# Two post-norm decoder layers on one core: the hand-written orders of the five engines replaced by a newly searched set

## The reference

```python
x = _layernorm(x + _L0_attn_ref(x, ...))            # 16 heads, window of 7 keys, a small net gives 7 weights a head
x = _layernorm(x + _L0_xattn_ref(x, ctx_1024, ...)) # one head, keys and values from ctx
x = _layernorm(x + _L0_ffn_ref(x, ...))             # 8 experts, each picks its 16 best tokens, attends among them
x = _layernorm(x + _L1_attn_ref(x, ...))            # one head of 256, scores times a decay mask
x = _layernorm(x + _L1_xattn_ref(x, ctx_1024, ...)) # argmax over ctx, then 16 heads over the chosen rows
x = _layernorm(x + _L1_ffn_ref(x, ...))             # quantised 256 -> 1024, width-3 convolution, silu, quantised back
```

## Time and profile before

| | |
|---|---|
| median of 3 executions | 1100.07 us (1093.01 to 1100.21) |
| the profiled execution | 1096.73 us, of it span 1094.9 us |
| TensorE matmul busy | 964.1 us (88%), 7038 instructions |
| TensorE weight load busy | 693.7 us (63%) |
| VectorE busy | 910.3 us (83%), 2503 instructions |
| ScalarE busy | 752.5 us (69%), 1854 instructions |
| GpSimd busy | 163.2 us (15%) |
| DMA queue of SyncE | 57.64 MB, 16.7% of 16 engines' time |
| mean granted TensorE clock | 0.947 |
| the chain that ended last | PE 68%, ACT 14%, DVE 12%, POOL 3%, issue 3% |

### The profile page before, as it was taken

One profiled execution on the slowest core, in us unless ns is written; L12 is line 12 of the kernel. 1 busy time (PEld: TensorE's weight loads), 2 busy tenths in 40 slices (PEclk: granted clock), 3 DMA queues, 4 the chain that ended last, 5 costly groups with the idle time before them and its releaser, 6 DMA issues.

```text
span 1094.9 us, 19705 instructions
## 1 busy us (share of the span) xinstructions
PE 964.1 (88%) x7038; PEld 693.7 (63%) x7038; DVE 910.3 (83%) x2503; ACT 752.5 (69%) x1854; POOL 163.2 (15%) x401
## 2 busy tenths in 40 slices
PE   5758889999999999999999999999999998887552
PEld 4536557676767676767767776768676756564331
DVE  4798776689898989898989989898999877867754
ACT  2223454768696878778787878786969795867643
POOL 2000110111112020302021211112120301010000
PEclk9878899999999999999999999999999998988865
DMA  7823021211110302030303020120212001000000
GB/s 224 325 67 106 1 87 34 63 46 42 49 58 9 98 21 86 6 101 1 106 1 90 17 81 26 45 63 20 77 40 68 10 1 30 1 20 1 10 10 10
DMA packets 36626, 58.90 MB, mean 54 GB/s; under 512 B 6784, under 2 KB 15872, under 8 KB 36016
## 3 DMA queue, kind: packets, MB, share of 16 engines
q1 hardware_dynamic: 36528, 57.64, 16.7%
HBM read 28.65 MB, written 4.19 MB: 30 GB/s over the span
## 4 chain that ended last, share of the span: by engine, by line
PE 68%; ACT 14%; DVE 12%; POOL 3%; issue 3%; DMA 0%; SPq 0%; ACTq 0%; POOLq 0%; DVEq 0%
PE bank_c L450 20%; PE bank_a L450 11%; PE banks_e L450 7%; PE bank_f L450 5%; PE bank_x L450 5%; PE bank_x L644 4%; PE bank_a L542 3%; PE bank_c L472 2%; ACT squares_out L1362 2%; ACT area_e L1559 2%; DVE x L880 2%; DVE area_a L1046 2%; PE banks_e L788 1%; PE banks_e L801 1%; ACT area_bx L1350 1%
## 5 line engine op out<-in xcount | busy, mean ns | idle before, releaser
L1284 DVE SCALAR_TENSOR_TENSOR area_f<-area_f,w_convw 128x254 f32<-128x254 f32 x256 | 111.5, 477 | 6.0 <-ACT area_f L1588 4.9
L1350 ACT ACTIVATE area_bx<-bank_x 128x512 f32<-128x512 f32 (+1 forms) x144 | 70.0, 498 | 29.3 <-PE bank_x L644 10.4
L1208 DVE TENSOR_REDUCE neg_top<-banks_e 128x8 f32<-128x1024 f32 x64 | 76.1, 1211 | 10.4 <-PE banks_e L450 10.3
L996 DVE TENSOR_TENSOR area_a<-area_a 128x512 f32<-128x512 f32 x112 | 73.4, 681 | 8.6 <-ACT area_a L1350 8.5
L1588 ACT ACTIVATE area_f<-area_f,w_convb,w_convw 128x256 f32<-128x256 f32 x128 | 69.6, 594 | 13.7 <-DVE area_f L1275 13.6
L1350 ACT ACTIVATE area_a<-bank_a 128x512 f32<-128x512 f32 (+1 forms) x80 | 44.1, 551 | 49.9 <-PE bank_a L450 28.3
L1350 ACT ACTIVATE area_bx<-bank_c 128x512 f32<-128x512 f32 x64 | 34.8, 544 | 61.3 <-PE bank_c L450 41.3
L1046 DVE TENSOR_TENSOR area_a<-area_a 128x512 f32<-128x512 f32 x112 | 74.4, 681 | 0.4
L1559 ACT ACTIVATE area_e<-banks_e 128x512 f32<-128x512 f32 x128 | 67.9, 599 | 1.3 <-PE banks_e L801 1.0
L1050 DVE TENSOR_TENSOR area_a<-area_a 128x512 f32<-128x512 f32 x96 | 65.1, 679 | 0.1
L1350 ACT ACTIVATE area_e<-banks_e 128x512 f32<-128x512 f32 (+1 forms) x80 | 45.8, 593 | 16.1 <-PE banks_e L472 5.9
(11 more groups left out here) (314 smaller groups left out, 2682.7 us busy)
## 6 DMA issues: line engine op xcount, KB each, us to landing
area_a<-area_a SPq DMA_DIRECT2D x96, 224.0 KB
area_a<-in_xT SPq DMA_DIRECT2D x16, 256.0 KB, 2.9
x<-in_x SPq DMA_DIRECT2D x16, 256.0 KB, 3.0
area_bx<-in_ctxT SPq DMA_DIRECT2D x16, 256.0 KB, 2.8
area_d<-in_ctxT SPq DMA_DIRECT2D x16, 256.0 KB, 3.0
y<-x SPq DMA_DIRECT2D x16, 256.0 KB, 2.2
w_wqkv_e<-in_wqkv_e SPq DMA_DIRECT2D x1, 3072.0 KB, 10.5
area_f<-in_raw SPq DMA_DIRECT2D x2, 1024.0 KB, 11.4
```

The costliest lines, as they stand in the source:

```text
L996: return dve.tensor_tensor(product_of(wi).rearrange("p (n t) -> p n t", t=P), qT0.rearrange("p c (b t) -> p (c b) t", t=P), kT0.rearrange( ...
L1208: dve.tensor_reduce(top[:, b, :, r:r + 2, 0].rearrange("p (par c) r -> p r c par", c=DC), banks_e[:, r:r + 2, :].rearrange("p r (c par k) ...
L1284: last = dve.scalar_tensor_tensor(c4[:, i, :, dst], h4[:, i, :, src], cwt3[:, 2 * jj + i, k:k + 1], c4[:, i, :, dst], ALU.mult, ALU.add)
L1350: return act.activation(dst, src, ACT.Copy)
```

## The change

The strings of `ORDER` are replaced for all five engines; the code of the steps, their waits, tiles and buffers stay as they are. The table's new rows, of which two stand for all:

```diff
 ORDER = {
     "PE": (
-        "AAAAASASSSSBBAAAABSABAABABBXXAASXBAAXAXBXBAAXXBBXXXXBSXABXXAASXBAXAXBXABBXAXCACXXXCXCXCCXACACXCACXACXCA"
+        "AAAAASASSBSSBAAAASBABABBAABXXAASXBAXAAXBAXABAXXBBXXXBXSXXABXASAXBAXAXBXABBXAXCACXXXCXCXCCCAXACXCACXACXCA"
...
     "SP": (
-        "ASSSSAAABSSSBSSAAABAAAACABAAAACABBACAFAAABCBCFAAACFBAAAFAAACBFBCAAAFBAAACFCBAAAFBAAACFAAACCBFBAACCFFCFFF"
+        "ASSSSSSAAABSBASASAABAABAACABAACACBAACAFBAACAFBAACAFAAABFAACABFBAACCAFAAABFAAACBFAAACBFAAABCFCAABCCCFFFFF"
```

More of the change, by code:

```diff
@@ new lines @@
+        "XFFAXAFAEAECXCAFCAAAFCAAAAAFEEAFAFFAAFFAFAFXECCCAFCFFFFFFEEXXXXXXAAXAXXFAEEEXFEEEFFBBAFFFAAFXXXXBBFFFFAA"
+        "FFXXAAFFEEACCFFAAAXFCCAAFAAAAFAFFAEXAEAAAAFCCCFFFEAFFCFFXXFXFFXXEXEXXXAAFXEFEFFAEEAEEBBFFXFFBAXAXAXBFFAA"
+        "XFFAXFAAAFFAFACCEFEFCAAXFCFAAAAAEFEAAFFAAXFAAFFFECCCAFFCFFFFFXXEEXXXXXEEXXEEFXEEAAFAFFABFXBFFFAAAXXXBBFF"
+        "AFFFAFFFXAXEAFFEACCAFACXAAAFCFAAAAAFFEEAXAAFAAAFFFECCCAFXFFFCXFFFXEEXXXXXXAAXFEEFAXFAFEEBBEEFAFFFBAAXXXF"
+        "BFFFAAXFAFFXAAAAFEAFECCFXAAAFCCAFAAFFFEAAAAEAFFAFAFEXCCCAFFFFCFFFXXXXEEAAAXXXAXXAFEEEXEFFFBXBEEFFBAAFFXX"
@@ new lines @@
+        "BXFFFFFFAAXXFAFAAFACCFEAEAFXACAACAAAAFEFEAFFAAAAXAFFFFECCCAFFFFCFFFXXXXEEAAXAXXXXFEEEXFEEEFFBAXBFFAFFAAX"
+        "XBXFBFFFAAFFFAXFAAAAXEECXCFFAAAFCCAAAAAFFFFEAEXAAAAAFFFFCCCEAFCFFFXXFXFXFEEXXAAXXXEEFEEXEEAFXFFFBBFAFAFX"
+        "BAXAXFBFFFFAAFXXAFAXAFEAEACCAFAAACCFAAAAFAAFAAAFEFFEXAFFFFCCCEAFCFXXFFXFFXXFXEEXXXEEFAAXEAFEFFAXBBEEFFAF"
+        "FBAAXXXBFFFFAAFFFXXEFFAAEACACAAFAAFXCCAFAAAFAAAFFXAEAEAAFFFFCCCEAFCFXXFFXFFXXFEEXXAAXXAAFXEEFEFFEEEFBXBF"
+        "AFFXXXFBAABFFFAXAFFFXFAAAEAAECCAFFAAXAFCCAAFAFFFAAAEEXAAFFAFAFECCCAFFFCFFFFXXXEEXXXAAXXXAFEEEXFAFFEEEFBB"
@@ new lines @@
+        "FBXCXCEXEEECEXCCECXCFFFAEFXXECXFACAAFFAFBFBBXAFFXBFEFXBFEEEFXACEFAFCBEXFCFXBXCECFEEEXCEXCCCEFCFFAFEXCEAX"
+        "XACAXFFFABFBFABXFFBXFEBXFFEEECEXAFFCFFAEXCXBFXCFBCXEEEECEXCCCECFFFAXEFXXCEAXFCAAFFAFBFBBXFFABXFEBFXFEEEE"
+        "AXCFFFCABECFFXBXCEXCFEEEXCEXCCCXECXXAFFFFECAEXCAAFFFABFBFBXAFFXFEBXFFBEEEEXACFFFECAXBCFXFBXCECXEEECXFECC"
+        "CCEXFAFFFCEXXECXAFAAFFFABFBBXAFFXBEFFBXFEEEEACXFFFECBFAXCFBXCXCFXECXEEECCECCXEAFXXFFFECAEXCFAAFBFAFBFBXA"
+        "FFXBFEXBFFEEEXAECFFFCBAEXCFXFBXCEECFXEEXCECCCECFXAFFFEXXECAFCXAAFFAFBBFBXAFFXBEBFFXFEEEEAFXCFFAECBFXFCBX"
@@ L110 @@
+        "FXCCEEEEXCEXCCCXEFCFFAXXFECAECXFBFAFFBBXFXBEFFEEEEBXFFFEFXCBFFXCXEBFCFXEEXCEXCFECXCCEFCFFFEXCXEFCFFXCFCC"
+        "CFEXFEFEEXFFFXECFFFXFCEFXXFCXEEEECCEXFCFFXEFCEXCECXFCFFCFFCEFFEEEECEFCFFCEEEFECCFFCFEFCFECFFFCFEEFFFFFEF"
+        "FFEEEEFFFEFFEEEFFEFEEFFFFEEFFFFFFFFFFFFFFFFFFFFFF"
     ),
     "POOL": (
[L112 removed]
+        "ABABXABXCABCXEABCXEAFBCXEAFCBXEAFBCXEAFBCEXAFBCXEAFBCXEAFBCXEAFBCXEAFBCXEAFBCXEAFBCXEFCEXFCEFEFF"
```

57 lines of the change are left out of this document (19 added, 38 removed).

## The result

The changed kernel takes 1115.22 us, the median of 4 runs (1109.62 to 1119.47); the kernel before, run beside it, 1099.67 us (1093.01 to 1100.21). The ratio is 1.0153, with a 95% interval of 1.0113 to 1.0193: slower by 12 to 21 us. The profiled execution after took 1115.31 us, of it a span of 1113.5, which is 18.6 us more than the span of the earlier trace rows.

The account below looks back on a forecast made before the run. TensorE was taken to bound the middle, chains through ScalarE and VectorE the ends. +7.6 - 1.8 - 1.0 + 0 = +4.8 us on 1096.73 gave 1101.5; 3.3 us to the median made it 1105, range 1091 to 1117.

Parts of the forecast that it names:

- within one per cent: Whole kernel: the class of times within one per cent of the kernel before, given a chance of 0.60.
- The start: Setup: SyncE's 5.4 MB block ahead of ctxT makes TensorE wait until 37.2 us; +7.6 us, bounds +1 to +14.
- shift copies at 298 GB/s: SyncE's start: 1.55 MB of copies inside SBUF, 149 GB/s at a share of 0.50 taken as 298, needing 5.2 us.
- The 12.8 us: TensorE's start: its work from ctxT's landing at 37.2 us to the transposes, predicted to begin at 50.0 us.
- The sums of VectorE: Start: VectorE's window sums, behind the shifts, run from 35.9 to 44 us, covered by TensorE's later transposes.
- Nothing gives the start back: After the start: nothing later in the ramp waits for a load, so the +7.6 us stays.
- Tile-size changes: TensorE's whole order: 464 changes instead of 473, at 0.2 us each; -1.8 us at most.
- Short gaps: Whole order: about fifteen filled gaps, 10 us, against as many opened; -1.0 us, bounds -10 and +6.
- The drain: Last groups: feed-forward order unchanged, group 15's memory step held by half microseconds or hidden; 0 us.
- The loads hide: Rival, start: ctxT lands at 31.5 us, the start costs 1 us, filled gaps keep 10; 1089 us, chance 0.15.
- Only the shifts count: Rival, start: ctxT passes slow shifts and VectorE's sums, 3.7 us late, set the pace; 1101 us, chance 0.1.
- The start dearer: Rival, start: the wait for ctxT drops TensorE's clock for the work behind it; +12, 1112 us, up to 1118, chance 0.25.

Follow-up runs that it names:

- after_end_back: The changed kernel with all engines' orders from about 860 us to the end taken from the kernel before: 1111.68 us, ratio 1.0127.
- before_sp_moved: The kernel before with only SyncE's decay-bit and expert-weight loads moved ahead of x, shifts, xT and ctxT: 1104.93 us, ratio 1.0057.
- after_sp_back: The changed kernel with SyncE's first 12 steps in the order of the kernel before: 1106.36 us, ratio 1.0068.
- before_late_new: The kernel before with all engines' orders between about 560 and 860 us taken from the new order: 1101.55 us, ratio 1.0029.
- before_early_new: The kernel before with all engines' orders between about 60 and 560 us taken from the new order: 1096.34 us, ratio 0.9990.
- after_pe_back: The changed kernel with TensorE's first 13 steps in the order of the kernel before, SyncE's loads still late: 1113.73 us, ratio 1.0140.
- before_end_new: The kernel before with all engines' orders from about 860 us to the end taken from the new order: 1103.47 us, ratio 1.0053.
- before_pe_moved: The kernel before with only group 0's cross projection moved ahead of TensorE's third setup product and bias products: 1101.61 us, ratio 1.0018.

## Why the prediction was right and where it was wrong

The 1115.22 us lie within the range of 1091 to 1117, near its end, and 10 us above the predicted 1105; "within one per cent", my likeliest class, was wrong.

**The start: mechanism right, the shift copies mis-sized.** ctxT landed at 40.87 us where I had 37.2, and at 40.03, 42.26 and 40.69 in the three other traces with the late loads: all beyond my upper bound of 39.4. The first product came at 63.71 (63.10 in after_end_back, which has the same start) where I had 61.8. The term that failed is the shift copies at 298 GB/s. Stretches of the kernel after, columns of the earlier trace rows:

```profile
20.00:24.00 4.00, 0.96 (x9) 0.49 (x12) 3.64 (x9) 0.23 (x1) 0.00 (x0) 0.75 0.98 418
17.00:28.00 11.00, 7.11 (x42) 4.24 (x42) 8.77 (x21) 3.18 (x6) 0.00 (x0) 0.73 1.01 398
28.00:41.00 13.00, 2.96 (x12) 2.23 (x11) 7.67 (x20) 0.60 (x1) 0.00 (x0) 0.76 1.02 254
32.00:40.00 8.00, 0.00 (x0) 0.00 (x0) 2.95 (x9) 0.00 (x0) 0.00 (x0) 0.73 1.06 257
```

As long as only the block flows, up to 28 us, the queue moves 398 GB/s, so the 405 of my sum held. From 28 us on the shift copies share the queue with w_wo_e and x, and it moves 254 GB/s at a share just as full. A packet of 2 KB takes 0.09 us between 44 and 46 us of before, where only loads flow, and 0.13 to 0.15 between 32 and 38 us here. Those 13 us carry 3.3 MB. If the loads among them, 1.75 MB, went at 405 GB/s, the 1.55 MB of copies took 8.7 us and not 5.2, about 180 GB/s; that is an estimate, and its 3.5 us are nearly the whole 3.7 by which ctxT was late. So the step that failed is the doubling of 149 GB/s at half a share to 298 at a full one. The 12.8 us that I gave TensorE from ctxT to its transposes were 11.5, which brought 1.3 back. The sums of VectorE, predicted to be covered, were: they end at 47.9, TensorE is ready at 52.4.

What the start costs in the kernel's time can't be told apart from the predicted 7.6 us: 9.5 us by the first product in the two traces, 6.6 to 12.6 by the steps at 260 us with the spread above, and 6.3 for the loads alone by the time of before_sp_moved.

The Trainium skill ("DMA: Bandwidth & Descriptors", section "Where 436 GB/s comes from") puts about 358 GB/s for loads from HBM to one core. The 418 GB/s that this trace moves from 20 to 24 us, when w_wqkv_e flows, lies above it, and the measurement decides. The same section's 435 for copies inside SBUF isn't what this trace shows either: 257 GB/s at a full share of 1.06, with the copies in the queue.

**Nothing gives the start back: right.** +9.6 at 260 us and at 620 in after; 8.4 us between after and after_sp_back at 60 to 80 us, and 8.5 all the way from 260 to 920.

**Tile-size changes, -1.8: not seen.** Six changes fewer between 300 and 560 us, with 0.4 us less of waits beside them, gained nothing where 1.6 us were due. So waits didn't eat the saving: the 0.2 us a change, which came from one pair of rows, doesn't hold over this stretch. What a change costs isn't shown.

**Short gaps, -1.0: the wrong sign, and the step that failed in the middle.** I had counted filled gaps against opened ones and let the filled ones weigh more. Measured were 0 up to 560 us, +3.1 from there to 860 (before_late_new) and +1.2 more to 920. Filled gaps in the ramp were worth 2.6 us at 140 us and nothing at 260 in before_early_new; an opened one in the full middle stayed to the end. The bound of +6 held.

**The drain, 0: the other failed step.** I judged it by the steps' order. At the full clock the order is no dearer: after_sp_back even ends 1.8 us ahead of its place at 920 us. But at the lower level it costs 4.6 us (after) to 8.3 (after_pe_back), and which of the two comes differs between runs of one kernel. Over many executions it is dearer: before_end_new costs 5.8 us by its ten times (2.1 to 9.6). Behind 920 us the six traces with the new end lie between 1.8 us gained and 8.3 lost against before, the seven others with the old end between 1.7 gained and 2.3 lost. In after the clock fell behind a 2.17 us wait:

```profile
931.40 0.44 PE L477 MATMUL bank_c<-w_ident,area_c 128*128 128x128 f32 x2 [2.17 <-DVE area_c L1186]
...
939.20 3.78 PE L450 MATMUL bank_c<-area_c,w_qk 128*128 128x256 f32 x8 [0.69 <-ACT area_c L1350]
```

The same rows of after_sp_back, 8.5 us earlier, with the same wait and no fall:

```profile
922.87 0.44 PE L477 MATMUL bank_c<-w_ident,area_c 128*128 128x128 f32 x2 [2.17 <-DVE area_c L1186]
...
928.61 1.99 PE L450 MATMUL bank_c<-area_c,w_qk 128*128 128x256 f32 x8 [0.69 <-ACT area_c L1350]
```

In the order before, that wait is split in two, 1.27 and 0.27 us, with the product of wr_pad between, and there too the clock fell at 918 us; so I can't say that the order of this place invites it. Why the new end loses more by the clock stays open.

**The rivals.** "The loads hide" was wrong by its premise (12.1 us for ctxT). Its other leg fails too: the ten microseconds of filled gaps that it kept are not there in before_early_new, which is no faster than before. "Only the shifts count" was wrong: ctxT came behind them. "The start dearer" at 1112 came near the time by luck: the lower clock did follow the wait, for 5 us, but the output projection and the queries behind the transposes ran at the full one (1.99 and 1.97 us), and what it lacked was the middle and the drain.

**The pieces beside the whole.** By the ratios, in us of 1100: SyncE's loads 9.4 (1.0153 less 1.0068), TensorE's place 2.0 (taken from before_pe_moved), the stretch to 560 -1.1, to 860 +3.2, the end +5.8: 19.3, against 16.8 for the whole. The intervals of the single terms (2 to 5 us each side) cover the difference, and would cover a larger one.

## What to carry to other kernels

- A load moved ahead of others in a full queue delays each of them by its bytes at the rate of that stretch, and the first engine to need a late one stops with all that is queued behind it. Here that cost 8.5 us. An earlier place of the consumer adds to it only little: 3.1 us in the traces.
- The rate of a full queue depends on what is in it. Loads moved 398 GB/s here, loads with the shift copies among them 254. A rate read at half a share is no guide to the full one.
- Traces of one order can lie 6 us apart after the first 200 us. Compare two traces from a point on from which they run parallel.
- In a pipeline, a gain in the ramp lasts only until the bounding engine is full; a wait opened where that engine is full lasts to the end. Price a new order by the second kind.
- Orders of several engines are one plan. Half of a plan (13 and 11 us) says nothing of what the whole costs (3).

## What the runs showed of the hardware that was not expected

The clock of TensorE in a stretch with many short waits isn't a property of the order: two executions of one kernel, equal within 0.3 us up to 975 us, ended 7.2 us apart by it, and the ten times of before_end_new lay in two groups, 12.6 us from lowest to highest. The Trainium skill ("TensorE: Matmul & The Clock Gate", "Part 1: The HAM clock gate", section "What's actually happening") says that the window in which the clock is decided runs free of the kernel's start, and so one kernel varies between runs. The traces agree that it varies: with the same order and the same steps, the first fall behind 220 us came at 949 us in one trace of after_sp_back's kernel and at 1024 in the other. The page also puts the penalty of the ramp under 1% of a typical kernel. Here the clock in the drain was worth 0.65% between two executions, 7.2 us, more than the 3.1 us of the middle and little less than the start.

The start varies too: five traces with one start have the first product of group 1 between 52.07 and 57.29 us. In the trace of before the clock was at its lower level from 40.6 to 50.9 us, and the first product came at 54.19. In the two traces in which it was full from 37.5 to 64.8 us that product came at 52.07 and 52.24.
